# Attention inside a fused layer: three PSUM banks for the score products that feed the maxima, one bank in place of two for the value products

## What is computed

```python
q = (h @ Wq).reshape(Bb, Ss, H, Dh)          # Dh = 8, H = 16, Ss = 256
k = (h @ Wk).reshape(Bb, Ss, H, Dh)
v = (h @ Wv).reshape(Bb, Ss, H, Dh)
scores = jnp.einsum('bqhd,bkhd->bhqk', q, k) / jnp.sqrt(jnp.float32(Dh))
attn = jax.nn.softmax(scores, axis=-1)
ctx = jnp.einsum('bhqk,bkhd->bqhd', attn, v).reshape(Bb, Ss, Dd)
x = x + ctx @ Wo
```

## Time and profile before

| | us |
|---|---|
| timed runs | 1097.06, 1089.57, 1224.69 |
| median of the three | 1097.06 |
| the profiled execution, device time | 1081.27 |
| its span, first to last instruction | 1079.4 |
| PE busy (matmuls) | 792.2 |
| DVE busy | 813.8 |
| ACT busy | 589.7 |
| POOL busy | 529.8 |
| chain that ended last: PE, DVE, POOL | 57%, 19%, 9% |
| in it, line 1337 (PE) and line 1100 (DVE maximum) | 54%, 11% |

### The profile page before, as it was taken

How to read it: one execution, slowest core, us unless ns; L and a number is a source line. 1 busy time by engine, 2 the same in 40 slices (tenths; PEclk the granted TensorE clock), 3 DMA queues, 4 the chain that set the end, 5 groups by cost and what they waited for, 6 DMA issues and landing times.

```text
span 1079.4 us, 25392 instructions
## 1 busy us (share of the span) xinstructions
PE 792.2 (73%) x8366; PEld 489.8 (45%) x8367; DVE 813.8 (75%) x1600; ACT 589.7 (55%) x1198; POOL 529.8 (49%) x669
## 2 busy tenths in 40 slices
PE   3587566588888988888888888861999999995000
PEld 2355444223444434443334334441788888885000
DVE  7788689577886788888887878527888888888522
ACT  6754278436766677777546667740655555552000
POOL 9500099401225461615017486845677336665775
PEclk9999889868988899999768999975999999999555
DMA  7820023401111111211001221001455445543432
GB/s 183 314 84 1 1 79 117 161 26 46 46 50 38 43 47 51 61 31 32 16 26 44 59 58 56 22 20 32 112 137 132 114 107 130 134 125 97 131 82 71
DMA packets 132071, 84.16 MB, mean 78 GB/s; under 512 B 54520, under 2 KB 117628, under 8 KB 131982
## 3 DMA queue, kind: packets, MB, share of 16 engines
q1 hardware_dynamic: 123790, 66.20, 21.2%
q0 software_dynamic: 8192, 16.79, 5.8%
HBM read 30.25 MB, written 41.94 MB: 67 GB/s over the span
## 4 chain that ended last, share of the span: by engine, by line
PE 57%; DVE 19%; POOL 9%; issue 6%; ACT 3%; DMA 1%; SPq 0%; POOLq 0%; ACTq 0%; DVEq 0%
PE bank L1337 54%; DVE arena L1100 11%; POOL HT L757 3%; POOL Z L757 3%; DVE arena L1036 2%; POOL xh L501 1%; PE bank L1341 1%; POOL rr L497 1%; PE bank L1517 1%; PE bank L1524 1%; DVE Z L1020 1%; DVE mom L955 1%; DVE Z L1027 1%; ACT Z L806 1%; ACT arena L836 0%
## 5 line engine op out<-in xcount | busy, mean ns | idle before, releaser
L1100 DVE TENSOR_REDUCE arena<-bank 128x2 f32<-128x512 f32 x512 | 339.3, 688 | 97.0 <-PE bank L1337 94.9
L855 ACT ACTIVATE arena<-bank 128x512 f32<-128x512 f32 x512 | 292.8, 596 | 155.0 <-PE bank L1337 153.0
L1337 PE MATMUL bank<-QK 32*128 32x256 f16 (+1 forms) x2048 | 193.9, 291 | 79.0 <-DVE arena L1100 66.5
L1337 PE MATMUL bank<-w2p,QK 128*128 x1280 | 216.5, 246 | 1.4 <-DVE arena L1300 1.4
L928 ACT ACTIVATE arena<-bank,b1s 128x256 f32<-128x256 f32 x320 | 125.3, 475 | 102.7 <-PE bank L1337 99.0
L1337 PE MATMUL bank<-arena,w1h 128*128 128x256 f16 x640 | 165.3, 275 | 12.3 <-DMA arena<-expert_in 9.4
L689 POOL DMA_INDIRECT expert_in<-HT,idx x128 | 133.3, 1041 | 83.5 <-PE bank L1337 47.0
L1337 PEld LDWEIGHTS bank<-QK 32*128 32x128 f16 (+1 forms) x2048 | 59.8, 94 | 215.5 <-ACT arena L855 163.0
L1337 PE MATMUL bank<-arena,VA 128*32 128x256 f32 x2048 | 150.4, 415 | 0.7 <-ACT arena L855 0.7
L1337 PEld LDWEIGHTS bank<-w2p,QK 128*128 128x128 f16 x1280 | 124.0, 98 | 10.8 <-issue 1.7
L1295 DVE TENSOR_TENSOR QK<-arena,QK 128x1024 f16<-128x1024 f32 x80 | 98.0, 1225 | 2.7
(11 more groups left out here) (158 smaller groups left out, 1152.7 us busy)
## 6 DMA issues: line engine op xcount, KB each, us to landing
QK<-qk_parts SPq DMA_DIRECT2D x96, 128.0 KB, 2.6
expert_in<-arena SPq DMA_DIRECT2D x40, 256.0 KB, 3.1
expert_out<-arena SPq DMA_DIRECT2D x80, 128.0 KB
qk_parts<-arena SPq DMA_DIRECT2D x16, 512.0 KB, 2.8
X<-x SPq DMA_DIRECT2D x8, 512.0 KB, 5.7
wst<-w SPq DMA_DIRECT2D x16, 256.0 KB, 2.8
out<-arena SPq DMA_DIRECT2D x16, 256.0 KB, 2.6
expert_in<-HT,idx POOLq DMA_INDIRECT x128
```

Source lines behind the costliest of these rows:

```text
L855: nc.scalar.activation(PT[t % 8], bank[2 + t % 2][:, :], ACT.Exp, scale=DH ** -0.5)\
L1100: V.tensor_reduce(nmax[n % 2][:, :, 4 * j + g], bank[u % 2][:, :].rearrange("p (q t) -> p q t", q=2), AX.X, ALU.max, negate=True).then_inc ...
L1337: return nc.tensor.matmul(dst, lhsT, rhs, start=start, stop=stop)
```

## The change

- S products rotate over banks 0, 1 and 2 (`u % 3`); before step t PE waits for the maximum of step u - 3 in place of u - 2. DVE reads the same banks.
- ST products move from banks 2 and 3 to 3 and 4. Their wait is as before.
- The value products of every sequence go to bank 5. The first of them in a sequence waits for the copy to `CT` of the sequence just before (`ct_ready >= b`), where it waited for the one before that.
- Ahead of the lead PE also waits for `v3_ready >= NG - 1`, the copy of the last projection of v that used bank 2.

No instruction is added, and none changes its place.

```diff
@@ exp_step (ACT)
-                nc.scalar.activation(PT[t % 8], bank[2 + t % 2][:, :], ACT.Exp, scale=DH ** -0.5)\
+                nc.scalar.activation(PT[t % 8], bank[3 + t % 2][:, :], ACT.Exp, scale=DH ** -0.5)\
@@ ctx_evac (ACT)
-                copy(CT, bank[4 + b % 2][:, :].rearrange("p (a t) -> p a t", a=2)).then_inc(ct_ready, 1)
+                copy(CT, bank[5][:, :].rearrange("p (a t) -> p a t", a=2)).then_inc(ct_ready, 1)
@@ max_chunk (DVE)
-                                bank[u % 2][:, :].rearrange("p (q t) -> p q t", q=2),
+                                bank[u % 3][:, :].rearrange("p (q t) -> p q t", q=2),
@@ st_half, s_half (PE)
-                return mm(bank[2 + t % 2][:, SL * kt:SL * kt + SL], k[:, 1, P * kt:P * kt + P], k[:, 0, :])
+                return mm(bank[3 + t % 2][:, SL * kt:SL * kt + SL], k[:, 1, P * kt:P * kt + P], k[:, 0, :])
...
-                return mm(bank[u % 2][:, SL * qt:SL * qt + SL], k[:, 0, P * qt:P * qt + P], k[:, 1, :])
+                return mm(bank[u % 3][:, SL * qt:SL * qt + SL], k[:, 0, P * qt:P * qt + P], k[:, 1, :])
@@ s_waits (PE)
-                if u >= 2:
-                    pe.wait_ge(max_done, u - 1)
+                if u >= 3:
+                    pe.wait_ge(max_done, u - 2)
@@ pv (PE)
-                    if b >= 2:
-                        pe.wait_ge(ct_ready, b - 1)
+                    if b:
+                        pe.wait_ge(ct_ready, b)
...
-                        last = mm(bank[4 + b % 2][32 * j:32 * j + 32, SL * gp:SL * gp + SL],
+                        last = mm(bank[5][32 * j:32 * j + 32, SL * gp:SL * gp + SL],
@@ ahead of the lead (PE)
             pe.wait_ge(lo_ready, NG - 1)
+            pe.wait_ge(v3_ready, NG - 1)
```

## The result

The changed kernel takes 1052.3 us, the median of four runs (1046.5 to 1054.2), against 1093.3 us for the kernel before (four runs, 1081.7 to 1224.7). The execution of 1224.7 us was in a slower state than the others, and the ratio leaves it out. The ratio is 0.964, with a 95% interval of 0.958 to 0.970: faster by 3.6%. Run again later beside the kernel before it came to 0.957 (0.950 to 0.964). The forecast was 1064 us, in a range of 1046 to 1088, and faster.

What follows compares the result with a forecast made beforehand. Waits between engines bound the main loop, DVE's maximum ending last. 26.1 full-clock blocks x 0.88 = 23 us, plus 2.4 us in the lead, make 25 us off 1089.6: 1064 us, range 1046 to 1088.

Steps and rivals of the forecast that it cites:

- The bound: Main loop while S products run: PE waits on DVE's maximum, which ends last; the exponential's wait is close behind.
- The gain of a block: Main loop at full clock: a block of 13.8 us gains 0.88 us, summed over its four periods.
- The 0.06: Value products of c2 to those of c6: gain of only 0.06 us, since transposes wait for the copy to CT.
- Each 0.19: Places like c1 and c6 to c10: 0.19 us gained as the exponential's wait replaces the maximum's.
- each 0.31: Period c14 to c2, and c14 in blocks without transposes: weights could start 0.31 us earlier.
- The lead: S products ahead of the main loop: maxima 0.60 us apart instead of 0.70, 25 intervals, 2.4 us saved.
- What costs nothing: Added wait for v3_ready ahead of the lead and single value bank: both free, since earlier waits already cover them.
- The rule quoted against it: Independent matmul groups should rotate through banks; the single value bank would lose some 20 us, leaving about 5 us gain.
- Half clock and routing: Half-clock stretches of the main loop (81 us) and routing's 11 us at full clock: no gain counted.
- The rival on the clock: Main loop: PE falls to half clock more often and the kernel gets slower, 1124 us with 140 us more; chance 0.06.
- second rival: Main loop: the clock recovers, half of 54 us at half clock goes, 12 us more saved, 1052 us; chance 0.12.

Runs made afterwards that it cites:

- third-ST-bank kernel: Kernel before with the single value bank, ST products over three banks waiting for the exponential of t - 3, S keeping two banks and its old wait: ratio 0.996.
- the two kernels with short maxima: Kernel before and changed kernel, each with every maximum taken over only 128 of 256 keys: ratios to before 0.964 and 0.960.
- the short exponential: Changed kernel with each exponential over the first 256 of its 512 columns, which the value products read twice: ratio to before 0.947.
- second profile of before: Kernel before, unaltered, run and profiled once more: ratio 1.001, 1153 us.
- second profile of the changed kernel: Changed kernel, unaltered, run again beside the kernel before and profiled: 1044.4 against 1094.8 us, ratio 0.957.

## Why the prediction was right, and where it was off

**The bound.** Right: the maximum's wait ends last and the exponential's comes next. The third-ST-bank kernel shows the first half (41.7 us, nothing gained), the two kernels with short maxima show that one wait passes behind the other, and the short exponential shows which comes next.

**The gain of a block.** The term was 0.88 us; it came out as 1.05: blocks 10 to 13, one of each kind, took 55.6 us before and 51.4 after, 13.90 and 12.85 each. By four steps, from the starts of the exponentials:

```
steps      before         after          gain        kind of block
c0-c3      3.70 / 4.04    3.37 / 3.71    0.33        without / with logits after c3 of the block
c4-c7      3.43 / 3.49    3.37 / 3.26    0.06 / 0.23 the same
c8-c11     3.12 / 3.40    2.89 / 2.89    0.23 / 0.51 without / with statistics on DVE
c12-c15    3.54 / 3.22    3.31 / 2.89    0.23 / 0.33 with / without transposes after c13
```

The 0.06 was right. Each 0.19 came out as 0.23 and each 0.31 as 0.33. A part of that is seen in the rows: released by the maximum, the matmul started 0.03 us behind its weights (493.97 and 494.00); released by the exponential it starts with them (483.83 and 483.83). The larger miss is the block with statistics: DVE lagged there and held c8 to c11 0.28 us longer, which the third bank removes too. I had left that out; it is 0.28 us in every fourth block.

**The lead.** 2.4 us forecast, 3.1 measured. The changed lead's maxima:

```profile
211.48 4.28 DVE L1100 TENSOR_REDUCE arena<-bank 128x2 f32<-128x512 f32 x7 [5.18 <-PE bank L1337]
```

They are (4.28 - 0.69) / 6 = 0.60 us apart, as worked out from the earlier trace rows. Over the 25 intervals that makes 2.5 us (18.0 before, 15.5 after), as forecast. The other 0.6 us lie behind the last maximum of the lead: from its start to the first exponential it is 0.85 us before and 0.25 after. The first step of the main loop brings an S product with its own wait for a maximum, and I had counted the lead only up to there. With the wait relaxed in the lead alone these are 2.5 us and 0.85.

**What costs nothing.** Right for the value bank: 41.7 us for blocks 13 to 15, and no wait on the copy at the value products. Right for `v3_ready` too: the first product of the changed lead, at 210.87 us, is still released by the load of q and k, and its maximum starts at 211.48. The rule quoted against it from the Trainium skill (Perfetto Trace Analysis, Optimizing Tensor Performance, Matmuls) doesn't bite where another wait already orders the copy ahead.

**Half clock and routing.** Counted at nothing. From block 2 on that held at half clock: 29 steps of blocks 2 to 19 stand wholly at half clock in traces with the old wait and in traces with the new one, and take 37.0 and 36.7 us. It failed in block 0, where PE has less other work: wholly at half clock it took 17.35 us in the second profile of before and 16.16 in both profiles of the changed kernel, 1.2 us less. Which stretches are at half clock changes between executions. Routing gave 3.1 us in this pair, with 37.5 us at half clock before and 30.7 after. In the second profile of before, with 30.7 too, blocks 20 to 22 took 57.9 us, so about 2 us of the 3.1 are the third bank's and the rest may be clock. DVE is busiest there; that a deeper queue of products fills some of its pauses is argued.

**The rival on the clock.** From the first exponential to step 486, half clock takes 89 us in the trace of before and 94 in that of after; the second profile of the changed kernel has 77. The third bank brought no swinging of the clock: blocks 10 to 19 and 23 to 29 are at 1.00 in both profiles of the changed kernel. So the third rival didn't happen, and in this pair of profiles the second didn't either. But the medians differ by 41 and 50 us, where blocks (26 x 1.05), lead (3.1) and routing (2) account for 32.

The clocks of all runs of the second comparison say where the rest is. The five runs of the kernel before that its ratio counts were at half clock for 268 to 306 us of their span, the four of the changed kernel for 235 to 263, on average 44 us less. By a straight line through those five the time rises by 0.31 us with each microsecond of half clock, so the 44 us go with some 13. The means of these five and four differ by 46 us: 33 without the clock, which is what the terms give. This is the recovered clock of the second rival, which had 0.12 and named 1052 us, the time that was measured. It is a correlation over few runs, and no run shows why the changed kernel is at half clock for less time.

The forecast was 12 us too high, and its gain of 25 us fell short by 16, since it started from 1089.6 us and the kernel before took 1093.3. Of the 16 about 7 are the sizes of the terms (26 x 0.17, 0.7 and 2) and some 9 are left, for which the clock is the likeliest cause; the clocks of the timed runs of the kernel before are not on record for the first comparison. That 1052 lies in the range is in part luck: the range went down to 1046 for the clock's sake, and the misses of size and the clock went the same way.

## What to carry to other kernels

When two waits stand ahead of one instruction, take for each the end of the work that it waits for and add the release time seen where that wait stands alone; the larger one is the wait, the gap to the other is the gain, and nothing beyond it. Don't go by the name that the profile gives the wait of a weight load. Before giving a second bank away, look whether an earlier instruction in the same stream already waits for the copy out of it. Profile the kernel before twice as well: the stall in block 6 and the long stretch at half clock looked like the change's doing beside the first profile, and both stand in the second. Where single profiles don't add up to the medians, compare the granted clocks of all runs.

## What was not expected of the hardware

- The release of PE takes 0.11 us behind a maximum, whose wait is a separate instruction ahead of the weight load, and 0.05 us behind an exponential, whose wait is on the weight load itself.
- The clock fell to 1.2 GHz in the lead though PE's records there are busy 14.2 of 15.9 us, and also with 21.8 of 21.8 us busy; filling matmuls just ahead of it, at 2.4 GHz, didn't prevent that.
- The same kernel before took 1093 to 1095 us in two groups of runs and 1142 to 1152 in three. In a profile from the latter full-clock blocks take the same 13.9 us. What is longer is the part from block 23 on, and the stages behind attention (396.5 against 370.1 us). Blocks 23 to 29 take 125.7 us against 101.3; half clock, at 0.43 us for each of 44 us more, makes some 19 of these 24 (an estimate), and PE stands for up to 5 us at places that the trace gives no cause for. Each of the four later groups ran on a chip of its own, so a difference between chips is the nearest rival; nothing here tests it, and why is open.
